# Two attention layers on one core: the bf16 split of the minima goes to GpSimd, high halves are written by ScalarE

## The reference

```
layer 0: y = layernorm(x);  x = x + attention(y, y, key mask) @ Wo + bo;  x = x + context @ Wg + bg
         x = x + relu(layernorm(x) @ W1 + b1) @ W2 + b2
layer 1: x = x + attention(layernorm(x), itself, causal) @ wo
         x = x + attention(layernorm(x), context, no mask) @ wo
         z = layernorm(x);  out = x + relu(z @ w1 + b1) @ w2 + b2
```

## Time and profile before

| | |
|---|---|
| median of 3 runs | 1756.74 us (1756.67 to 1759.3) |
| profiled execution | 1759.88 us, its span 1757.8 us |
| mean granted TensorE clock | 0.939 of full |
| PE busy | 1485.4 us (85%), 13376 matmuls |
| DVE busy | 1438.7 us (82%), 4560 instructions |
| ACT busy | 939.3 us (53%), 1849 instructions |
| POOL busy | 730.6 us (42%), 612 instructions |
| DMA | 185.73 MB, 106 GB/s over the span |

### The profile page before, as it was taken

One profiled execution on the slowest core, in us unless ns is written; L12 is line 12 of the kernel. 1 busy time (PEld: TensorE's weight loads), 2 busy tenths in 40 slices (PEclk: granted clock), 3 DMA queues, 4 the chain that ended last, 5 costly groups with the idle time before them and its releaser, 6 DMA issues.

```text
span 1757.8 us, 42638 instructions
## 1 busy us (share of the span) xinstructions
PE 1485.4 (85%) x13376; PEld 1203.8 (68%) x13376; DVE 1438.7 (82%) x4560; ACT 939.3 (53%) x1849; POOL 730.6 (42%) x612
## 2 busy tenths in 40 slices
PE   2789999999999999677777777778889898998987
PEld 1568787888878887555655555556777776777756
DVE  2889888898988997787888788888888888888762
ACT  2666666666666654344444545454555545555451
POOL 3345444454544555423232222334444444444423
PEclk8799999999999999888898988899999999999998
DMA  5555445445544445454546464756444554445400
GB/s 139 135 120 130 106 96 114 103 108 118 116 114 96 121 96 129 104 120 96 120 103 116 100 117 107 138 114 118 99 95 92 113 112 92 93 100 112 88 25 12
DMA packets 163509, 185.73 MB, mean 106 GB/s; under 512 B 15952, under 2 KB 140240, under 8 KB 163408
## 3 DMA queue, kind: packets, MB, share of 16 engines
q1 hardware_dynamic: 163408, 184.57, 48.3%
HBM read 125.78 MB, written 58.72 MB: 105 GB/s over the span
## 4 chain that ended last, share of the span: by engine, by line
PE 55%; DVE 24%; issue 11%; POOL 3%; ACT 2%; DMA 2%; DVEq 1%; SPq 1%; ACTq 0%
PE d_ps L436 25%; PE d_ps L672 7%; PE o_ps L571 6%; DVE prob L849 6%; PE s_ps L493 6%; PE t_ps L507 4%; PE t_ps L541 4%; DVE top_rest L862 2%; PE m_ps L443 2%; POOL k_f L1062 2%; DMA k_stack<-parts 1%; DVE prob_t L1022 1%; DVE stats L871 1%; DVE o_q L911 1%; DVE k_part L934 1%
## 5 line engine op out<-in xcount | busy, mean ns | idle before, releaser
L720 ACT ACTIVATE prob_t<-t_ps 128x384 f32<-128x384 f32 (+1 forms) x512 | 275.7, 545 | 416.2 <-PE t_ps L541 212.6
L493 PE MATMUL s_ps<-k_stack,q_stack 96*128 96x256 bf16 (+1 forms) x1536 | 298.1, 277 | 102.5 <-DVE top L849 42.4
L711 ACT ACTIVATE prob<-prob,neg_max 128x256 f32<-128x256 f32 x512 | 233.0, 505 | 194.7 <-DVE neg_max L849 192.0
L493 PEld LDWEIGHTS s_ps<-k_stack,q_stack 96*128 96x128 bf16 x1536 | 116.2, 101 | 211.7 <-DVE top L849 66.0
L541 PE MATMUL t_ps<-q_stack,k_stack 108*128 108x256 bf16 (+1 forms) x1024 | 214.2, 276 | 8.7 <-ACT q_stack L728 8.6
L1062 POOL TENSOR_TENSOR h_lo<-h_f,h_hi 128x512 fp32r<-128x512 f32 x128 | 167.6, 1309 | 128.6 <-DVE h_hi L949 128.6
L849 DVE CUSTOM_DVE_ANT_0 prob<-s_ps,bias_sb 128x256 f32<-128x256 f32 x512 | 192.9, 416 | 22.0 <-PE s_ps L493 13.7
L571 PE MATMUL o_ps<-prob_t,v_sb 128*17 128x256 f32 (+1 forms) x3072 | 197.7, 377 | 0.0
L834 DVE TENSOR_REDUCE top<-s_ps 128x2 f32<-128x512 f32 x256 | 171.3, 680 | 23.0 <-PE s_ps L493 23.0
L728 ACT ACTIVATE q_stack<-o_ps 12x1024 bf16<-12x1024 f32 x128 | 130.2, 1017 | 106.7 <-PE o_ps L520 105.0
L849 DVE CUSTOM_DVE_ANT_0 prob<-s_ps,causal 128x128 f32<-128x128 f32 (+1 forms) x512 | 156.9, 349 | 34.6 <-PE s_ps L493 33.7
(11 more groups left out here) (113 smaller groups left out, 4148.3 us busy)
## 6 DMA issues: line engine op xcount, KB each, us to landing
q_stack<-parts SPq DMA_DIRECT2D x288, 128.0 KB, 4.1
k_stack<-parts SPq DMA_DIRECT2D x288, 128.0 KB, 6.4
parts<-q_part SPq DMA_DIRECT2D x96, 192.0 KB, 2.3
parts<-k_part SPq DMA_DIRECT2D x96, 192.0 KB, 2.3
ct_kept<-ct_hl SPq DMA_DIRECT2D x16, 512.0 KB, 7.7
x_in<-x_mid SPq DMA_DIRECT2D x32, 256.0 KB, 2.8
x_res<-x_mid SPq DMA_DIRECT2D x32, 256.0 KB, 2.9
ct_hl<-ct_kept SPq DMA_DIRECT2D x16, 512.0 KB, 8.0
```

The costliest lines, as they stand in the source:

```text
L493: last = mm(s_ps[:, h % 2, q * S:q * S + n], q_stack[0:ROWS, t.par, HEAD[h], q * P:(q + 1) * P], k_stack[0:ROWS, t.par, HEAD[h], 0:n], sta ...
L711: last = nc.scalar.activation(prob[:, h % 4, q, :], prob[:, h % 4, q, :], ACT.Exp, bias=neg_max[:, h % 4, q:q + 1], scale=-1.0)
L720: nc.scalar.activation(prob_t[:, h % 8, 0:n], t_ps[:, h % 2, 0:n], ACT.Exp, scale=-1.0)\
```

## The change

Four things are changed. The arithmetic that gives each value is the same.

1. `top_split` moves from DVE's queue to POOL's, in the same slots. All that follows in passes 1 and 2 moves one slot on: PE's `top_rows` and ACT's `top_copies` (`R_LAG` 6 for `CH + 1`, which is 5), the keyed scores (`T_LAG` 7 for 6), their exponentials (`E_LAG` 8 for 7) and `values` (`PV_LAG` 12 for 11).
2. The high halves of x, x2 and the context, and part 0 of q and k, are written by ACT straight from PSUM: each eviction is done twice, first into the high part, then into the float32 tile. DVE's five casts are gone. POOL's subtractions wait for ACT.
3. ACT takes over the waits that guarded those tiles (parts written, context stored, projections read).
4. The division, transpose and `ot` split (`NORM_AT`) move from slots 9 and 10 to 6 and 7 in pass 0, and to 10 and 11 in passes 1 and 2.

```diff
-T_LAG, E_LAG = 6, 7
-PV_LAG = (8, 11, 11)
+R_LAG, T_LAG, E_LAG = 6, 7, 8
+PV_LAG = (8, 12, 12)
 V_AT = 10
+NORM_AT = (6, 10, 10)
...
-                t, ht = head_at(st, h, CH + 1, KEYED)
+                t, ht = head_at(st, h, R_LAG, KEYED)
                 if t and ht % CH == 0:
                     top_rows(st, t, ht // CH)
...
-            def affine(dst, col_g, col_b, done):
+            def affine(high, dst, col_g, col_b, done):
-                for k in range(KC):
-                    last = nc.scalar.activation(dst[:, k, :], m_ps[:, k * S:(k + 1) * S], ACT.Identity,
+                for out_t in (high, dst):
+                    for k in range(KC):
+                        last = nc.scalar.activation(out_t[:, k, :], m_ps[:, k * S:(k + 1) * S], ACT.Identity,
...
-                    affine(tf_b, c, c + 2, x2t_f)
+                    affine(x2t_hi, tf_b, c, c + 2, x2t_f)
...
+                        act.wait_ge(q_written.of(st.cur), q_written.after(st.cur))
+                    act.sem_inc(passed, 1)
+                    for dst in (q_part[:, 0], q_f[:, :, :]):
...
+                    for dst in (k_part[:, 0], k_f[:, :, :]):
...
+                    nc.scalar.activation(ct_hi[:, :, :], turned, ACT.Copy)
+                    nc.scalar.activation(tf_b[:, :, :], turned, ACT.Copy).then_inc(ct_f.sem, 1)
...
+                        act.wait_ge(v_mm.sem, v_mm.after(st.nxt))
-                    affine(tf_a, c, c + 2, xt_f)
+                    affine(xt_hi, tf_a, c, c + 2, xt_f)
...
-                if h == 9 and has(st.prev):
+                if has(st.prev) and h == NORM_AT[st.prev.p]:
                     dve.wait_ge(o_done.sem, o_done.after(st.prev))
...
-                    v.tensor_copy(x2t_hi[:, :, :], tf_b[:, :, :]).then_inc(x2t_h.sem, 1)
-                    v.tensor_copy(q_part[:, 0], q_f[:, :, :]).then_inc(q_p1.sem, 1)
-                    v.tensor_copy(k_part[:, 0], k_f[:, :, :]).then_inc(k_p1.sem, 1)
-                    v.tensor_copy(ct_hi[:, :, :], tf_b[:, :, :]).then_inc(ct_h.sem, 1)
-                    v.tensor_copy(xt_hi[:, :, :], tf_a[:, :, :]).then_inc(xt_h.sem, 1)
...
+            def top_split(st, t, c):
+                pool.wait_ge(u_done.sem, u_done.after(t, CH * (c + 1)))
+                before, cb = (t, c - 2) if c >= 2 else (st.prev if t is st.cur else st.old, c + 2)
+                if has(before, KEYED):
+                    pool.wait_ge(top_mm.sem, top_mm.after(before, cb + 1))
+                src, part = top[:, c % 2], top_part[:, c % 2]
+                g.tensor_tensor(part[:, :, :, 0], src, zeros[:, :, :], ALU.add).then_inc(top_1.sem, 1)
+                pool.wait_ge(top_1.sem, top_1.after(t, c + 1))
+                g.tensor_tensor(top_rest[:, :, :], src, part[:, :, :, 0], ALU.subtract).then_inc(top_r.sem, 1)
+                pool.wait_ge(top_r.sem, top_r.after(t, c + 1))
+                g.tensor_tensor(part[:, :, :, 1], top_rest[:, :, :], zeros[:, :, :], ALU.add).then_inc(top_2.sem, 1)
+                pool.wait_ge(top_2.sem, top_2.after(t, c + 1))
+                g.tensor_tensor(part[:, :, :, 2], top_rest[:, :, :], part[:, :, :, 1], ALU.subtract)\
+                    .then_inc(top_3.sem, 1)
...
             def slot(st, h):
+                t, ht = head_at(st, h, CH, KEYED)
+                if t and ht % CH == 0:
+                    top_split(st, t, ht // CH)
                 if h == 15 and has(st.nxt2):
-                    pool.wait_ge(xt_h.sem, xt_h.after(st.nxt2))
+                    pool.wait_ge(xt_f.sem, xt_f.after(st.nxt2))
```

More of the change, by code:

```diff
@@ L758, in slot @@
                         act.wait_ge(q_p3.sem, q_p3.after(st.cur))
[L759 to L765, removed]
+                        act.wait_ge(q_written.of(st.cur), q_written.after(st.cur))
+                    act.sem_inc(passed, 1)
+                    for dst in (q_part[:, 0], q_f[:, :, :]):
+                        if st.nxt.p == 0:
+                            for m in range(KC):
+                                last = nc.scalar.activation(dst[:, m, :], d_ps[:, 1, m * S:(m + 1) * S], ACT.Identity,
+                                                            bias=cols_sb[:, C_BQ + m:C_BQ + m + 1], scale=-0.25)
+                        else:
+                            last = nc.scalar.activation(dst, d_ps[:, 1, :].rearrange("p (m s) -> p m s", m=KC),
+                                                        ACT.Copy, scale=-0.25)
                     last.then_inc(q_done.sem, 1)
@@ L770, in slot @@
                         act.wait_ge(k_p3.sem, k_p3.after(st.cur))
[L771 to L777, removed]
+                        act.wait_ge(k_written.of(st.cur), k_written.after(st.cur))
+                    act.sem_inc(passed, 1)
+                    for dst in (k_part[:, 0], k_f[:, :, :]):
+                        if st.nxt.p == 0:
+                            for m in range(KC):
+                                last = nc.scalar.activation(dst[:, m, :], d_ps[:, 0, m * S:(m + 1) * S], ACT.Identity,
+                                                            bias=cols_sb[:, C_BK + m:C_BK + m + 1])
+                        else:
+                            last = nc.scalar.activation(dst, d_ps[:, 0, :].rearrange("p (m s) -> p m s", m=KC),
+                                                        ACT.Copy)
                     last.then_inc(k_done.sem, 1)
@@ L851, in score_guard @@
                 last.then_inc(u_done.sem, 1)
[L853 to L867, removed]
             def statistics(src, st_t, done):
@@ L911, in slot @@
                     v.transpose(o_q[:, c].rearrange("p b w -> p (b w)"), o_ps[:, 0:S]).then_inc(o_done.sem, 1)
-                if h == 10 and has(st.prev):
+                if has(st.prev) and h == NORM_AT[st.prev.p] + 1:
                     dve.wait_ge(o_norm.sem, o_norm.after(st.prev))
@@ L917, in slot @@
                                 o_n[:, :].rearrange("p k b w -> p (k b w)")).then_inc(ot_f.sem, 1)
-                if h == 3 and has(st.old, MLP):
-                    dve.wait_ge(x2t_f.sem, x2t_f.after(st.old))
-                    v.tensor_copy(x2t_hi[:, :, :], tf_b[:, :, :]).then_inc(x2t_h.sem, 1)
                 if h == 3 and has(st.nxt, (0,)):
```

57 lines of the change are left out of this document (19 added, 38 removed).

## The result

The changed kernel takes 1708.3 us (median of 4 runs, 1704.1 to 1721.1) against 1756.7 us: ratio 0.974, 95% interval 0.968 to 0.980. The forecast was 1674, so it gained 48 us where 83 were forecast. The profiled execution took 1704.1 us, 55.8 less than that of before.

What follows compares the result with a forecast made beforehand. Bound: TensorE and DVE waiting on each other, DVE in pass 1 with a DMA loop close under. Sixteen steps each, 0 - 46 - 37 = -83 us, from 1759.9 to 1677, less 3.1 for the median: 1674 us; range 1620 to 1730.

Steps and rivals of the forecast that it cites:

- The bound: What limits each pass: pass 0 close to TensorE's own work, pass 1 DVE, pass 2 in between.
- the DMA loop: Pass 1: scores, projections, q and k split, DMA, next scores; 27.8 us, 1.3 under the step of 29.1.
- Part 1: Split of the minima leaves DVE: 3.9 us a step in pass 1, 5.7 in pass 2; on Pool 1.2 each.
- The slow-Pool rivals: Small Pool instructions cost like the pow (1722 us, chance 13%) or like a full subtraction (1795 us, chance 5%).
- Part 2: One more slot of lag in passes 1 and 2: moved work keeps its distances, no wait changes by itself.
- Part 3: High halves on ACT: DVE loses 2.0 to 3.0 us; stalls 1.9 in pass 0, 0.9 and 0.8 in pass 2.
- Part 4: Earlier norm in pass 0: moves 2 to 3 us of DVE work to slots 6 and 7, letting 1.8 of waits go.
- pass 0: Step change: -1.8 us of waits for DVE, +1.9 at the first MLP product, +0.1, taken as 0.
- -1.8 (waits for DVE): Pass 0: TensorE's waits for the minima from DVE, 1.8 us a step, were to go.
- Pass 1: Step falls 2.9 us to 26.2, set by the loop through DMA, with 1.6 less before the q parts leave.
- Pass 2: TensorE gets back at most its idle 4.0 us a step and pays new stalls of 0.9 and 0.8: -2.3.
- The rival of ACT's queue: ACT's in-order queue, slots 2 to 5 and 14, becomes the bound: +1.9 us a step, 1787 us; chance 6%.

Runs made afterwards that it cites:

- pool_only: The kernel before with only the split of the minima moved to Pool; lags, norm and casts as before: 1751.7 us, ratio 0.997.
- lag_only: The kernel before with only the extra slot of lag in passes 1 and 2; split and casts stay on DVE: 1727.3 us, ratio 0.984.
- split_only: The kernel before with the split on Pool and the extra slot of lag; DVE casts all high halves, pass 0 norm in slot 9: 1697.3 us, ratio 0.966.
- undo_norm: The changed kernel with the norm of pass 0 put back in slot 9: 1716.7 us, ratio 0.978.
- p0_on_dve: The changed kernel with DVE again casting all high halves in pass 0, norm kept in slot 6: 1699.0 us, ratio 0.965.
- act_only: The kernel before with only the high halves written by ACT; split on DVE, no extra slot, old norm: 1774.9 us, ratio 1.011.

## Why the prediction was right, and where not

**The bound** was read rightly: DVE in pass 1 with the DMA loop close behind. The two halved-load runs show both halves of it.

**Part 1** was right in size. A small Pool instruction takes 0.20 to 0.21 us, as in the tile's rows of after; one split goes from 987.75 to 988.81, 1.06 us where 1.2 were said. The slow-Pool rivals are out. DVE fell by 6.0 us in pass 1 (said: 6) and by 6.5 in pass 2 (said: 8). The 6.0 is partly luck: in pass 1 pool_only, which moves the split alone, has DVE at 20.1 us, 3.7 less (said 3.9), but 1.0 of the rest is one small instruction of the norm (`ve`) that takes 0.17 us instead of 1.18 wherever the slot is there, lag_only too, and was in no sum.

```profile
L1043 POOL TENSOR_TENSOR top_part<-top,zeros x128: 202/210/396, 661.9 to 1650.5; 128x8 bf16<-128x8 f32 x128
```

**Part 2** is the step that failed: "keep their distances to each other, so none of these waits changes by itself". The distances within the moved chain stayed, but those to the work that did not move changed. In pass 2 ACT's copy went behind the last relu, whose wait of 1.6 us a step went; the slot alone was worth 1.1 us a step there, and with the split most of the 2.3 (without it after has 36.2). In pass 1 a chunk of values went behind the first scores, into the loop.

**Part 3.** The stalls were priced well: 1.68 us at the first MLP product of pass 0 (said 1.9), 0.8 in slot 5 of pass 2 (said 0.9), 0.7 in slot 0 (said 0.8). split_only has none of them; in pass 2 it has one wait of 1.2 us a step for the split on Pool instead, and its step is 33.5 against 34.0.

**Part 4 and pass 0** (said 0, came +1.0 a step, 16 us). The term "-1.8 (waits for DVE)" was mis-sized: 15.3/13.75 = 1.1 us of them are left, so 0.7 was given back. The waits of after add up to the rest: +1.6 for `k_f`, +0.5 for the relu, -0.4 for `prob_t`, with the -0.7 together +1.0. And the early norm is not what let the 0.7 go: it is the same in undo_norm. Its multiplications also took longer. The groups of DVE in pass 0, before and then after:

```profile
L900 DVE TENSOR_TENSOR o_n<-o_q,rden 128x256 f32<-128x256 f32 x28 | 10.7, 422 | 0.5
```

```profile
L890 DVE TENSOR_TENSOR o_n<-o_q,rden 128x256 f32<-128x256 f32 x28 | 27.9, 1036 | 1.0
```

In slot 6 the two multiplications meet Pool's subtractions of 1.2 to 1.3 us and take 0.6 us longer each, 1.2 a step. With the norm in slot 9 again (undo_norm) they take 422 ns as before, and DVE's busy time is 31.5 us a step, some 2.4 under before: that is most of why it fell by 1.1 us in pass 0 and not by 3. The Trainium skill, "SBUF — State Buffer", section "SBUF: two separate sides", says that DVE and GpSimd hold their shared port exclusively for a whole instruction; these rows agree. The 16 small Pool instructions, of which the prediction weighed the same rule, cost DVE nothing that can be seen in pass 1: between before and pool_only no other group of DVE's instructions there changes by more than 0.1 us a step.

**Pass 1** (said -2.9, came -2.3, 10 us). The loop was the limit, but its front part was mis-sized: from the first scores to the q parts 11.6 us where 10.5 (12.1 - 1.6) were said, for the values and the lower clock behind the wait. The back part was 15.6 (said 15.7). Both are means over the steps whose first scores waited, so they add up to more than the mean step. Between executions of the same pass 1 code the step ranges from 26.8 to 27.6 (after, p0_on_dve, undo_norm), and I have not found what decides that. The clock is a part of it: single steps of after take from 24.4 to 31.0 us, and the two shortest are the only ones at the full clock. This is one of them:

```profile
1008.64:1033.29 24.65, 19.96 (x222) 14.92 (x222) 17.80 (x86) 14.95 (x28) 10.15 (x22) 1.00 0.54 125
```

**Pass 2** (said -2.3, came -2.3) was right in number for a partly wrong reason, which is luck. The rise in ACT's stalls (0.5 against split_only) was paid by the relu's wait, which the prediction had named and not connected with the change.

The terms miss by 16 + 10 = 26 us; 7 us more lie between the medians and the profiled executions (1708.3 against 1704.1 after, 1756.7 against 1759.9 before), and the rest is rounding. The rival of ACT's queue was right in mechanism; all its cost less what it gives back in pass 1 is 11 us, after against split_only (1708.3 - 1697.3), and it did not decide the sign. Alone, in act_only, it made the kernel slower.

## What to carry to other kernels

A slot of lag added to cover a latency also moves every instruction of the chain past those that stand still, on each engine; list for each of them what it now stands ahead of and behind, above all the evictions for which TensorE waits and the work that fills a DMA wait. Test such parts in a square (neither, each, both): here they gave 7 and 31 us alone and 59 together. When a step is bound by a loop through DMA, work moved from ahead of the wait to behind it is paid in full, and again where the clock is lower behind the wait. Look at the clock of each step before a difference of means is put down to the edit.

## What the runs showed of the hardware

Halving a stack load from 128 to 64 KB cut its landing from 6.4 to 2.2 us, to a third and not to half. The six k loads are issued within 2.7 us, less than one of them takes to land, so they are in flight together, and the share of the DMA engines stands at 0.98 while PE waits in the window from 977.90; that they wait for each other there is an inference. A small Pool instruction (8 columns) takes 0.21 us, and dependent ones start 0.28 to 0.29 us apart. A 3.0 us idle time of TensorE was followed by some 3.9 us at 0.50 to 0.67 of the clock, one of 1.31 us in another kernel by none; one of 1.69 us in pass 0 of undo_norm was followed by 4 us at 0.57 to 0.61 in four steps and by the full clock in others.
